# Attention over cached keys and values: the products with the new values of four heads joined into one product of 512 columns

## The reference, cut to what matters

```python
k_all = jnp.concatenate([kc, k], axis=1)      # 512 cached keys, 32 new ones
v_all = jnp.concatenate([vc, v], axis=1)
scores = jnp.einsum('bqhd,bkhd->bhqk', q, k_all) * SCALE
scores = jnp.where(valid[:, None, None, :], scores, -1e+30)
probs = jax.nn.softmax(scores, axis=-1)
o = jnp.einsum('bhqk,bkhd->bqhd', probs, v_all)
```

## Time and profile before

| | |
|---|---|
| median of three runs | 3391.04 us (3390.39 to 3391.32) |
| the profiled execution | 3392.49 us, its span 3390.7 us |
| PE busy | 3281.0 us, 97% of the span |
| PE weight loads | 3026.4 us, 89% |
| DVE busy | 2257.2 us, 67% |
| ACT busy | 1763.5 us, 52% |
| POOL busy | 1338.1 us, 39% |
| granted TensorE clock, mean | 0.987 |

### The profile page before, as it was taken

How to read it: one execution, slowest core, us unless ns; L and a number is a source line. 1 busy time by engine, 2 the same in 40 slices (tenths; PEclk the granted TensorE clock), 3 DMA queues, 4 the chain that set the end, 5 groups by cost and what they waited for, 6 DMA issues and landing times. The chain is left out here.

```text
span 3390.7 us, 69362 instructions
## 1 busy us (share of the span) xinstructions
PE 3281.0 (97%) x22398; PEld 3026.4 (89%) x22398; DVE 2257.2 (67%) x6132; ACT 1763.5 (52%) x4307; POOL 1338.1 (39%) x2391
## 2 busy tenths in 40 slices
PE   7799999999899999999899999999999999999999
PEld 5688899987778888888899999999999998888878
DVE  6445644445478787788888888878888886323274
ACT  4323322233337788888666666666666665322222
POOL 0231100000017888888566666656666663100002
PEclk9899999999999999999999999999999999999999
DMA  5413422334645555556766666656666675533353
GB/s 207 136 58 71 127 82 80 86 105 144 208 143 184 173 170 175 185 175 207 244 219 221 213 221 220 220 186 216 217 221 219 213 231 189 173 106 102 114 184 103
DMA packets 448050, 571.93 MB, mean 169 GB/s; under 512 B 171657, under 2 KB 330185, under 8 KB 430794
## 3 DMA queue, kind: packets, MB, share of 16 engines
q1 hardware_dynamic: 427978, 429.08, 39.8%
q0 software_dynamic: 19712, 138.42, 11.6%
HBM read 394.60 MB, written 172.75 MB: 167 GB/s over the span
## 5 line engine op out<-in xcount | busy, mean ns | idle before, releaser
L2623 PE MATMUL l2a_x<-l2a_pt,l2a_V 128*128 128x128 f32 x4096 | 542.0, 275 | 0.8 <-DVE l2a_pn L2557 0.8
L2623 PEld LDWEIGHTS l2a_x<-l2a_pt,l2a_V 128*128 128x128 f32 x4096 | 498.6, 192 | 1.1 <-issue 1.1
L2535 DVE CUSTOM_DVE_ANT_0 l2a_sm<-l2a_s,l2a_B 128x544 f32<-128x544 f32 x512 | 370.2, 723 | 153.1 <-PE l2a_s L197 144.7
L2344 POOL CAST l2a_K<-cache 128x256 fp32r x768 | 306.9, 449 | 226.6 <-issue 226.6
L2489 ACT ACTIVATE l2a_p<-l2a_sm,l2a_st 128x544 f32<-128x544 f32 x512 | 379.8, 742 | 25.5 <-DVE l2a_st L2535 25.3
L2344 POOL CAST keys<-cache 128x256 fp32r x750 | 303.2, 451 | 175.2 <-issue 175.2
L2475 ACT ACTIVATE l2a_pt<-l2a_t 128x512 f32<-128x512 f32 x512 | 305.6, 597 | 102.1 <-PE l2a_t L2606 102.0
L2606 PE MATMUL l2a_t<-ident,l2a_p 128*128 128x128 f32 x2048 | 307.4, 273 | 5.2 <-ACT l2a_ao L2482 5.2
L2482 ACT ACTIVATE l2a_ao<-l2a_x 128x128 f32<-128x128 f32 x512 | 142.2, 278 | 279.7 <-PE l2a_x L2624 279.7
L2547 DVE TENSOR_SCALAR l2a_p<-l2a_p,l2a_st 128x512 f32<-128x512 f32 x512 | 270.7, 529 | 18.3
L197 PE MATMUL l2q_pa<-keys,cache 128*128 128x512 f32 (+1 forms) x1024 | 266.6, 342 | 3.4 <-DVE head L143 3.4
(11 more groups left out here) (855 smaller groups left out, 8592.3 us busy)
## 6 DMA issues: line engine op xcount, KB each, us to landing
s_qT<-l2q_qo SPq DMA_DIRECT2D x128, 512.0 KB, 2.8
head<-s_qT SPq DMA_DIRECT2D x64, 512.0 KB, 6.0
l2a_Q<-s_qT SPq DMA_DIRECT2D x64, 512.0 KB, 5.3
s_ao<-l2a_ao SPq DMA_DIRECT2D x64, 512.0 KB, 6.1
l2o_a<-s_ao SPq DMA_DIRECT2D x128, 256.0 KB, 3.0
s_kn<-l2q_ko SPq DMA_DIRECT2D x128, 128.0 KB, 2.9
head<-s_kn SPq DMA_DIRECT2D x32, 512.0 KB, 6.0
wqraw<-in_wqkv SPq DMA_DIRECT2D x32, 384.0 KB, 3.7
```

What stands on the lines that cost most here:

```text
L2344: e.tensor_copy(K[:, j:j + 1, :, :].rearrange("p a z n -> p a (z n)"), Kall[:, bass.ds(v, 1), :, :].rearrange("p a z n -> p a (z n)")).the ...
L2535: dve.tensor_tensor_reduce(out=smr[sc % 2][:, :], in0=ps_s[sc % 2][:, 224:768], in1=Br[g % 2][:, :], scale=-SCALE, scalar=3e38, op0=ALU.ad ...
L2623: pe.matmul(px[:, P:256], V[:, k * D + hg * P:k * D + hg * P + P], pt[:, k, :], start=k == 0, stop=False)
```

## The change

The four products with the new values (one a head, eight matmul instructions of 128 columns in all) become one product of 512 columns a group, in three parts. The stationary operand is the tile of new values itself, [128, 128], all four heads below each other; the moving operand is a tile `dg` of [128, 512], zero except for four blocks of 32 rows x 128 columns on its diagonal, one a head. ACT writes the high parts of the four blocks straight from the PSUM bank into which PE turned the new probabilities, DVE writes the rests. The bank of a group now holds 4 x 128 columns, and ACT takes it out once a group with one instruction of 512 columns.

ACT also makes the high part of the new values, in iteration 4(g+1), and waits there for the four loads; POOL makes the rest (`low_values`). The turning of the new probabilities moves from unit tr to unit pv, one iteration later. The copy of the new keys and the mask are now in different iterations.

```diff
-    Nr = st.slots("vn", 2, [P, 4, P], each=4)
+    Nr = st.slots("vn", 2, [P, P], each=4)
+    VN = [st.pair(f"vnew{i}", [P, P]) for i in range(2)]
+    dg = st.sb("diag", [P, 2, D], F32R)
+    corner = [(slice(32 * h, 32 * h + 32), slice(P * h, P * h + P)) for h in range(4)]
...
# SP
                 if g >= 2:
-                    sp.wait_ge(pv_mm, 4 * (g - 1))
-                else:
-                    sp.wait_ge(cleared, g + 1)
+                    sp.wait_ge(values_lo, g - 1)
...
-                    sp.wait_ge(o_copied, pv + 1)
+                    sp.wait_ge(o_copied, pv // 4 + 1)
...
# POOL
+            def low_values(g):
+                pool.wait_ge(values_hi, g + 1)
+                low_part(pool, [z[:, :] for z in VN[g % 2]], Nr[g][:, :]).then_inc(values_lo, 1)
...
+                if hg == 2 and g:
+                    low_values(g - 1)
...
# ACT, between the copy of the turned probabilities and the exponentials
-                    act.wait_ge(pv_mm, pv + 1)
-                    if pv % 8 == 0 and k >= 2:
-                        act.wait_ge(*ao.landed(k - 2))
-                    act.activation(ao[k][:, hg, :, 32 * (g % 2):32 * (g % 2) + 32],
-                                   ps_x[pv % 2][:, P:256].rearrange("p (h s) -> p h s", h=4), ACT.Copy).then_inc(o_copied, 1)
+                    if hg == 0:
+                        act.wait_ge(new_turned, g + 1)
+                        if g:
+                            act.wait_ge(new_mm, g)
+                        else:
+                            act.wait_ge(cleared, 1)
+                        for at, to in corner:
+                            m = act.activation(dg[at, 0, to], ps_x[(g + 1) % 2][at, 0:P], ACT.Copy)
+                        m.then_inc(new_hi, 1)
+                    if hg == 3:
+                        act.wait_ge(new_mm, g + 1)
+                        if g % 2 == 0 and k >= 2:
+                            act.wait_ge(*ao.landed(k - 2))
+                        act.activation(ao[k][:, :, :, 32 * (g % 2):32 * (g % 2) + 32].rearrange("p g h s -> p (g h) s"),
+                                       ps_x[g % 2][:, :].rearrange("p (h s) -> p h s", s=32), ACT.Copy).then_inc(o_copied, 1)
+                if i % 4 == 0 and 4 <= i <= U:
+                    g = i // 4 - 1
+                    act.wait_ge(*Nr.landed(g))
+                    if g >= 2:
+                        act.wait_ge(new_mm, g - 1)
+                    act.activation(VN[g % 2][0][:, :], Nr[g][:, :], ACT.Copy).then_inc(values_hi, 1)
...
# DVE
-                if tr is not None and tr % 4 == 0:
-                    g = tr // 4
-                    dve.wait_ge(new_turned, g + 1)
-                    if g >= 2:
-                        dve.wait_ge(pv_mm, 4 * (g - 1))
-                    dve.tensor_copy(pnr[g % 2][:, :], ps_x[tr % 2][:, 0:P]).then_inc(new_copied, 1)
+                if pv is not None and pv % 4 == 0:
+                    g = pv // 4
+                    dve.wait_ge(new_hi, g + 1)
+                    for at, to in corner:
+                        m = dve.tensor_tensor(dg[at, 1, to], ps_x[(g + 1) % 2][at, 0:P], dg[at, 0, to].bitcast(F32), ALU.subtract)
+                    m.then_inc(new_lo, 1)
...
                         if hg == 2:
+                            new_keys(n)
+                        if hg == 3:
                             mask(n)
...
# PE
-                        pe.wait_ge(o_copied, tr - 1)
...
-                    if hg == 0:
-                        pe.wait_ge(newed, tr + 4)
-                        pe.transpose(ps_x[tr % 2][:, 0:P], pNr[g % 3][:, :], ident[:, :]).then_inc(new_turned, 1)
...
                     if hg == 0:
+                        pe.wait_ge(newed, pv + 4)
+                        if g:
+                            pe.wait_ge(o_copied, g)
+                        pe.transpose(ps_x[(g + 1) % 2][:, 0:P], pNr[g % 3][:, :], ident[:, :]).then_inc(new_turned, 1)
+                        if g:
+                            pe.wait_ge(new_lo, g)
...
                         pe.wait_ge(*Vr.landed(g))
-                        pe.wait_ge(*Nr.landed(g))
-                        pe.wait_ge(new_copied, g + 1)
...
-                        pe.matmul(px[:, P:256], V[:, k * D + hg * P:k * D + hg * P + P], pt[:, k, :], start=k == 0, stop=False)
-                    pe.matmul(px[:, P:256], vn[:, hg, :], pnr[g % 2][:, :], start=False, stop=True).then_inc(pv_mm, 1)
+                        m = pe.matmul(px[:, P * hg:P * hg + P], V[:, k * D + hg * P:k * D + hg * P + P], pt[:, k, :],
+                                      start=hg + k == 0, stop=False)
+                    m.then_inc(pv_mm, 1)
+                    if hg == 3:
+                        pe.wait_ge(new_lo, g + 1)
+                        pe.wait_ge(values_lo, g + 1)
+                        mm3(pe, px[:, :], [([z[:, :] for z in VN[g % 2]], (dg[:, 0, :], dg[:, 1, :]))], start=False).then_inc(new_mm, 1)
```

More of the change, by code:

```diff
@@ L2306, in l2_attn @@
     ptr = [st.sb(f"pt{i}", [P, 4, P]) for i in range(2)]
-    pnr = [st.sb(f"pn{i}", [P, P]) for i in range(2)]
     str_ = [st.sb(f"st{i}", [P, 8]) for i in range(4)]
@@ L2312, in l2_attn @@
     inverted, scaled, newed = (st.sem(n) for n in ("inverted", "scaled", "newed"))
-    turned, new_turned, t_copied, new_copied, pv_mm, o_copied = (
-        st.sem(n) for n in ("turned", "new_turned", "t_copied", "new_copied", "pv_mm", "o_copied"))
+    turned, new_turned, t_copied, new_hi, new_lo, pv_mm, new_mm, o_copied, values_hi, values_lo = (
+        st.sem(n) for n in ("turned", "new_turned", "t_copied", "new_hi", "new_lo", "pv_mm", "new_mm", "o_copied", "values_hi", "values_lo"))
     change = {4 * (NB - 2) + 2: 4, 4 * (NB - 2) + 3: 5, 4 * (NB - 1): 6, 4 * (NB - 1) + 2: 7}
@@ L2383, in fetch_new_values @@
                 if g >= 2:
-                    sp.wait_ge(pv_mm, 4 * (g - 1))
-                else:
-                    sp.wait_ge(cleared, g + 1)
+                    sp.wait_ge(values_lo, g - 1)
                 for h in range(4):
-                    sp.dma_start(Nr[g][32 * h:32 * h + 32, h, :],
+                    sp.dma_start(Nr[g][32 * h:32 * h + 32, :],
                                  S["vn"][b * 32:(b + 1) * 32, (4 * half + h) * P:(4 * half + h + 1) * P]).then_inc(Nr.sem(g), 16)
@@ L2428, in low @@
                 low_part(pool, chunk_tiles(n), stage[n % 3][0][:, :, :]).then_inc(chunk_g, 1)
-            for z in Nr.bufs:
-                pool.memset(z[:, :, :], 0.0).then_inc(cleared, 1)
+            pool.memset(dg[:, :, :].bitcast(F32), 0.0).then_inc(cleared, 1)
             def values(g):
@@ L2455, in _ @@
                     page_copies(pool, r, n, range(10, 16), pages_g)
+            low_values(G - 1)
         @block.scalar
@@ L2512, in mask @@
                 half, b = divmod(g, NB)
-                if g:
-                    new_keys(g)
                 if g >= 2:
@@ L2584, in _ @@
                         if sc > LV:
-                            pe.wait_ge(o_copied, sc - LV)
+                            pe.wait_ge(new_lo, (sc - LV) // 4 + 1)
                         keep_busy(pe, ps_x[1][:, 0:P], ident[:, :], fill[sc])
@@ L2607, in _ @@
                     m.then_inc(turned, 1)
-                    if hg == 0:
-                        pe.wait_ge(newed, tr + 4)
-                        pe.transpose(ps_x[tr % 2][:, 0:P], pNr[g % 3][:, :], ident[:, :]).then_inc(new_turned, 1)
                 if pv is not None:
                     g, hg = divmod(pv, 4)
[L2613 to L2616, removed]
+                    V, pt, px = Vr[g], ptr[pv % 2], ps_x[g % 2]
                     if hg == 0:
+                        pe.wait_ge(newed, pv + 4)
[4 more added lines that the diff above has]
+                            pe.wait_ge(new_lo, g)
+                        if pv == U // 2 - 8:
+                            keep_busy(pe, px[:, 0:P], ident[:, :], 15)
                         pe.wait_ge(*Vr.landed(g))
-                        pe.wait_ge(*Nr.landed(g))
-                        pe.wait_ge(new_copied, g + 1)
                     pe.wait_ge(t_copied, pv + 1)
                     for k in range(4):
-                        pe.matmul(px[:, P:256], V[:, k * D + hg * P:k * D + hg * P + P], pt[:, k, :], start=k == 0, stop=False)
-                    pe.matmul(px[:, P:256], vn[:, hg, :], pnr[g % 2][:, :], start=False, stop=True).then_inc(pv_mm, 1)
+                        m = pe.matmul(px[:, P * hg:P * hg + P], V[:, k * D + hg * P:k * D + hg * P + P], pt[:, k, :],
[5 more added lines that the diff above has]
+                        mm3(pe, px[:, :], [([z[:, :] for z in VN[g % 2]], (dg[:, 0, :], dg[:, 1, :]))], start=False).then_inc(new_mm, 1)
     st.mem.close()
```

## The result

The changed kernel takes 3503.52 us (median of 4 runs, 3496.27 to 3505.97) against 3391.18 us in runs of the kernel before beside it: 1.0325 times as long, 95% interval 1.0307 to 1.0344, 112 us more. The forecast was 3424 us with a range up to 3446. The side was right, the size was three times too small.

A forecast was written before the change was run, and what follows sets the result against it. PE sets the pace before; afterwards a ring through the loads' landing loses 0.57 us in 60 pairs, 34 us, with -2 and +1 at the edges: +33 on 3392.5 is 3425.5, median 3424 us, range 3384 to 3446.

The forecast's parts named there:

- PE's part: PE, per group: 0.89 us of matmuls removed, 0.68 added; gain 0.21, or 18.37 a pair for PE alone.
- The ring: Cycle landing, ACT, PE, ACT, store, landing: 19.36 us per two groups against 18.79; the likeliest case, chance 0.70.
- The parting of keys and mask costs nothing: DVE: separating keys and mask moves 0.5 us to the next iteration at no cost.
- two heads 4.20: PE's stretch after the new turning and V matmuls: two heads take 4.20 us of PE's 5.20.
- Store to landing: 8.3: SP's queue, odd groups: new-value loads land 8.3 us after the output store's issue.
- I keep 8.3: Store to landing stays 8.3 us although the gather goes out some 0.9 us ahead; 7.9 to 8.6 allowed.
- The forecast 33: Whole kernel: total predicted loss of 33 us, from ring +34, pairs outside it -2, last store +1.
- DVE "hidden": DVE's net +0.6 to +0.85 us a group fits in 1.12 of room, so it costs no time.
- DVE becomes the bound: Rival: DVE sets 9.47 us a group, +10 us, 3401 us; chance 0.04.
- The corners: Four corner copies on ACT at 0.16 us each, at most 0.28; four DVE subtractions 0.89 with the last's tail.
- The clock: Rival: PE's clock falls in each 1.0 us stall, 60 x 1.44 us more, 3510 us; chance 0.03.
- Expected signs: Stores 19.3 to 19.4 us apart; ACT idle some 170 us for `l2a_vn`, PE about 60 for `l2a_ao`; even groups none.

The follow-up runs named there:

- e7: Changed kernel with new keys ahead of the corners, loads ahead of the store, and one 128-row corner instead of four on ACT and DVE (output wrong): 3365.2 us, 0.9920.
- e1: Changed kernel with DVE copying the new keys ahead of the four corner subtractions, same iteration: 3466.6 us, 1.0213 to the kernel before.
- e6: Changed kernel with one corner instruction of 128 rows in place of four on ACT and DVE, output not the reference's: 3510 us in a single run.
- e11: As e1, with the mask made on POOL instead of DVE: 3463.4 us, 1.0206 to the kernel before.
- e10: As e1, with all but the last two output stores issued from ACT's queue: 3429.4 us, 1.0102 to the kernel before.
- e3: Changed kernel with new keys ahead of the corners and new-value loads ahead of the store: 3427.5 us, 1.0094 to the kernel before.
- third edit: On top of e3, POOL makes the mask instead of DVE: 3378.9 us, 0.9955 to the kernel before, whole computation done.
- e9: As e1, with POOL gathering half of the bytes of the values, output not the reference's: 3458.3 us, 1.0188 to the kernel before.

## Why the prediction was right in direction and wrong in size

- **PE's part held.** Three matmuls 0.23 apart; 18.39 a pair in e7 against 18.37.
- **The ring held, term by term, where it was worked out from code and rows.** 2.15 for 2.14, 3.70 for 3.67, and medians of 11.06 and 11.07 for 11.01 in e1, e6 and e11. ACT waited 161 us for 170. e10 shows that the order in SP's queue makes the wait, and e11 that the ring sets the pace.
- **"The parting of keys and mask costs nothing" was the step that failed worst.** I counted the work and not its place: the keys stayed in iteration 4g+2, and the corners were put ahead of them in it. DVE reaches the corners only after ACT has made its four. PE wants the keys at the start of the next group. This raised "two heads 4.20" to 4.93: 11.83 - 11.01 = 0.82 a pair, 0.82 x 60 = 49 us. e1 gave back 37 by the order alone (by the mean intervals of the two profiles, 20.53 and 20.05, it is 29).
- **"Store to landing: 8.3" was misread in the kernel before.** "First store: last load issued 1667.3, landed 3.6 later" takes the shortest of the four times in the earlier trace rows for that of the last load. The view of that load alone says 4.5:

```profile
L2388 SPq DMA_DIRECT2D l2a_vn<-s_vn x1: 421/421/421, 1667.3 to 1667.3; - x1
DMA to landing us min/median/max: 4.5/4.5/4.5
```

So it landed 9.4 us after the store's issue, not 8.5. Read in this way, all 63 stores of the kernel before give 7.9 to 9.8, 8.8 on the mean, and with the shortest time 8.34. In the change ACT's copy starts 8.70 after the store on the mean, so the landing did not grow: "I keep 8.3" was right to keep it and kept the wrong number. 8.70 - 8.35 = 0.35 a pair, 0.35 x 60 = 21 us. The gather goes out 1.08 ahead of the store (0.9 forecast) and did the landing no visible harm. The forecast 33 and these two terms make 103, the growth of the span 103.8.

- **DVE "hidden" held only under the ring.** With the keys ahead of the corners and the loads ahead of the store DVE sets 19.46 a pair (e3), above the 18.79 of before. The rival "DVE becomes the bound" had the right mechanism and a price of 9.47 us a group that is 9.73. So the change as written had two ways to lose, and removing the one that I forecast would not have made it win.
- **The corners were priced from instructions of 128 rows.** ACT's four take 1.09 us, not 0.64, and DVE's 1.19, not 0.89.
- **The clock** didn't fall in the stalls: 1.00 in the stretch above.
- **Expected signs.** PE idle before the new turning, ended by `l2a_ao`, did come, but with 25.1 us and not 60. More is put down to DVE's `l2a_pnew` (34.1 us ahead of the weight load of that turning) and to the keys: ACT's lateness reaches PE through DVE too.

## What to carry to other kernels

When an instruction is inserted into an in-order engine, list everything behind it in the same iteration and when each is wanted, also what the change leaves where it was: "total work fits in the idle time" says nothing about that. A ring that passes through a DMA needs the landing of the last load, and a view that gives least, median and most of four loads does not say which is the last one's: ask for that load alone. Small loads wanted soon belong ahead of a big store in a queue, or in another queue. After a loss is explained, remove it and look what the next limit is; here it was again above the old time, and only the third edit gave a gain.

## What the runs showed of the hardware

Copies of a 32-row corner out of the bank are as long as those of all 128 rows. On DVE the four of 32x128 take 1.19 us, 0.29 each, and the single 128x128 of e6 takes 0.28:

```profile
1907.40 0.28 DVE L2574 TENSOR_TENSOR l2a_diag<-l2a_x,l2a_diag 128x128 fp32r<-128x128 f32 x1
1907.60 0.28 DVE L2529 CAST l2a_K<-head 128x256 fp32r<-128x256 f32 x1
```

Nor do they overlap: the four corners start 0.30 apart, where the next instruction starts 0.20 after the single one of e6, and the 128-row ones of the earlier trace rows, which read no bank, came 0.20 apart too.

DVE's instructions are longer beside POOL's. In the changed kernel, while POOL copies pages and before it does:

```profile
1903.72 0.48 DVE L2567 TENSOR_SCALAR l2a_p<-l2a_p,l2a_st 128x512 f32<-128x512 f32 x1
1904.12 0.23 DVE L2570 TENSOR_SCALAR l2a_pnew<-l2a_p,l2a_st 128x32 f32<-128x32 f32 x1
...
1906.79 0.70 DVE L2567 TENSOR_SCALAR l2a_p<-l2a_p,l2a_st 128x512 f32<-128x512 f32 x1
1907.41 0.37 DVE L2570 TENSOR_SCALAR l2a_pnew<-l2a_p,l2a_st 128x32 f32<-128x32 f32 x1
1907.69 0.69 DVE L2537 TENSOR_SCALAR l2a_B<-l2a_iota,seq 128x544 f32<-128x544 f32 x1
```

and POOL's row of that time:

```profile
1905.37 4.84 POOL L2346 CAST keys<-cache 128x256 fp32r x12 [2.57 <-issue]
```

The mask took 0.50 before in an iteration without POOL's pages and takes 0.69 in the one that it was moved to. So moving work also changed its price. The Trainium skill ("SBUF — State Buffer", section SBUF: two separate sides) calls the port pair that VectorE and GpSimd share an exclusive lock, which VectorE takes for instructions in a two-port mode or with two SBUF inputs, and which is held for a whole instruction. The rows agree that the two hinder each other; they don't show in which mode these instructions run, nor whether it is by that lock.

What stands around the loads sets when they land. Behind the store in SP's queue ACT's copy starts 8.7 us after the store on the mean in the change, 8.8 in e1 and e11 and 9.4 in e6; in the kernel before the loads land after 8.8. With the store in ACT's queue they land after 6.8 (e10), with half of the gathered bytes after 6.7 (e9). The gather's lead over the store (0.06 us before, 1.08 in the change, 0.79 in e1, 0.92 in e11) shows no effect; why e6, with 0.49, is later is open.
